# Second attention block: both halves of the head mix written into one bank, back to back, with one reciprocal and one product on VectorE

## The reference, cut to what matters

```python
wq = (q @ wq_w.T + wq_b).reshape(b, t, H, DH)          # H = 16, DH = 8
wk = (k @ wk_w.T + wk_b).reshape(b, t, H, DH)
wv = (v @ wv_w.T + wv_b).reshape(b, t, H, DH)
scores = jnp.einsum('bthd,bshd->bhts', wq, wk) / jnp.sqrt(jnp.float32(DH))
probs = jax.nn.softmax(scores, axis=-1)
attn = jnp.einsum('bhts,bshd->bthd', probs, wv)
return attn.reshape(b, t, d) @ wo_w.T + wo_b
```

## Time and profile before

| | before |
|---|---|
| median of 3 runs | 430.23 us |
| the profiled execution | 430.68 us |
| its span (first to last instruction) | 428.9 us |
| TensorE matmul busy | 383.9 us, 90% |
| VectorE busy | 332.2 us, 77% |
| ScalarE busy | 255.9 us, 60% |
| GpSimd busy | 226.7 us, 53% |
| mean granted TensorE clock | 0.976 |

### The profile page before, as it was taken

How to read it: one execution, slowest core, us unless ns; L and a number is a source line. 1 busy time by engine, 2 the same in 40 slices (tenths; PEclk the granted TensorE clock), 3 DMA queues, 4 the chain that set the end, 5 groups by cost and what they waited for, 6 DMA issues and landing times. The chain is left out here.

```text
span 428.9 us, 10603 instructions
## 1 busy us (share of the span) xinstructions
PE 383.9 (90%) x3641; PEld 282.8 (66%) x3654; DVE 332.2 (77%) x933; ACT 255.9 (60%) x506; POOL 226.7 (53%) x372
## 2 busy tenths in 40 slices
PE   8799989999999999999999999988888887765765
PEld 7356656666666666786578887856666766654554
DVE  3789998999989998885738874665588888866772
ACT  2478757777777777766542224445777676773252
POOL 4575497566666666632300002773788887656021
PEclk9999999999999999999999999999999999975799
DMA  5889999100000000000000000000000000000011
GB/s 160 245 146 136 135 125 127 14 3 2 2 2 2 2 2 2 0 2 2 2 2 0 0 2 2 0 2 2 2 2 3 2 2 2 2 2 0 16 38 49
DMA packets 61284, 13.29 MB, mean 31 GB/s; under 512 B 51488, under 2 KB 60592, under 8 KB 61232
## 3 DMA queue, kind: packets, MB, share of 16 engines
q1 hardware_dynamic: 59776, 11.94, 18.8%
q10 hardware_dynamic: 1328, 0.66, 0.5%
q0 software_dynamic: 128, 0.00, 0.0%
HBM read 11.55 MB, written 1.05 MB: 29 GB/s over the span
## 5 line engine op out<-in xcount | busy, mean ns | idle before, releaser
L397 POOL TENSOR_TENSOR a_rn<-a_ssq,neghalf 128x8 f32<-128x8 f32 x48 | 79.0, 1655 | 30.1 <-DVE a_ssq L996 25.6
L996 DVE TENSOR_REDUCE a_ssq<-q_home 128x8 f32<-128x512 f32 x48 | 32.3, 673 | 6.4 <-ACT q_home L783 6.3
L486 PE MATMUL a_x<-wkv_a,a_kvT 128*128 128x512 f32 x64 | 34.5, 621 | 0.9 <-ACT kv_home L789 0.8
L91 POOL TENSOR_TENSOR moments<-moments,eps_row 128x1 f32<-128x1 f32 x32 | 6.2, 195 | 54.9 <-DVE moments L86 54.6
L789 ACT ACTIVATE kv_home<-a_x,maskcol 128x512 f32<-128x512 f32 x32 | 21.9, 684 | 18.4 <-PE a_x L486 18.4
L1750 DVE TENSOR_REDUCE b_mx<-b_s 128x16 f32<-128x1024 f32 x16 | 19.6, 1225 | 10.4 <-PE b_s L1461 10.3
L1338 POOL TENSOR_TENSOR b_k<-b_ksb,quad 128x256 f32<-128x256 f32 x32 | 19.0, 614 | 14.3 <-ACT b_ksb L1625 14.3
L1015 DVE TENSOR_REDUCE a_mx<-a_s 128x4 f32<-128x512 f32 x32 | 22.0, 686 | 2.0 <-PE a_s L512 1.9
L413 POOL TENSOR_TENSOR a_yr<-a_ymv,eps_row 128x1 f32<-128x1 f32 x16 | 3.1, 192 | 38.0 <-DVE a_ymv L1039 38.0
L801 ACT ACTIVATE kv_home<-a_m,cols 128x512 f32<-128x512 f32 x32 | 22.0, 686 | 0.8 <-PE a_m L500 0.7
L531 PE MATMUL a_m<-kv_home,p_home 128*64 128x65 f32 x512 | 22.0, 228 | 0.3 <-ACT p_home L811 0.3
(11 more groups left out here) (293 smaller groups left out, 1186.7 us busy)
## 6 DMA issues: line engine op xcount, KB each, us to landing
w_gu<-in_L_ffn_Wg_dram SPq DMA_DIRECT2D x4, 512.0 KB, 9.1
w_gu<-in_L_ffn_Wu_dram SPq DMA_DIRECT2D x4, 512.0 KB, 11.1
w_d<-in_L_ffn_Wd_dram SPq DMA_DIRECT2D x8, 256.0 KB, 7.8
out_dram<-xs SPq DMA_DIRECT2D x8, 128.0 KB, 1.8
xs<-in_x_dram SPq DMA_DIRECT2D x1, 640.0 KB, 11.4
cs<-in_ctx_dram SPq DMA_DIRECT2D x1, 640.0 KB, 10.9
wkv_a<-in_L_xattn_Wkv_dram SPq DMA_DIRECT2D x1, 512.0 KB, 8.4
nat<-in_L_ffn_w_dram SPq DMA_DIRECT2D x2, 256.0 KB, 3.1
```

Of the source, the lines that this page charges most:

```text
L397: nc.gpsimd.tensor_tensor(rn[:, tp, i, :], ssq[:, tp, i, :], neghalf[:, 0:H0], ALU.pow)\
L486: nc.tensor.matmul(p_x[:], kvT[:, tp, b * 2 * S:(b + 1) * 2 * S], wkv_a[:, INNER:2 * INNER], start=True, stop=True).then_inc(vproj_done, 1)
L996: nc.vector.tensor_reduce(ssq[:, tp, i, :], sq[:, i, :].rearrange("p (h d) -> p h d", h=H0), AX.X, ALU.add).then_inc(reduced, 1)
```

## The change

Three edits go together. On TensorE, `mix(t, 1)` moves from behind `project` of the next turn to directly behind `mix(t, 0)`, and writes the same bank `p_m`, in the columns behind the first half (2 x 72 = 144 of 512). The waits that guarded `p_y` go: three in `mix(t, 1)`, one in `up`. On VectorE, `attend` waits once, for both halves, and then takes one reciprocal over 16 columns and one product over 128, where it took two of each over 8 and 64.

```diff
             def mix(t, tp, j):
                 pe.wait_ge(prT_ready, 2 * t + j + 1)
                 pe.wait_ge(v_ready, 2 * t + 2)
-                if j == 1:
-                    wait(pe, x_new, t)
-                    wait(pe, hid_ready, t - 3)
-                    wait(pe, att_ready, t)
...
-                        last = nc.tensor.matmul(p_mix[j][b * S:(b + 1) * S, i * W:(i + 1) * W],
+                        last = nc.tensor.matmul(p_m[b * S:(b + 1) * S, n * W:(n + 1) * W],
...
             def up(t, tp):
                 pe.wait_ge(hT_ready, t + 1)
-                pe.wait_ge(att_ready, min(t + 4, NT))
...
                 if s >= 2 and exists(s - 1, NT):
                     project(s - 1, (s - 1) % 2)
-                if exists(s - 3, NT):
-                    mix(s - 3, (s - 3) % 2, 1)
...
                 if exists(s - 2, NT):
                     mix(s - 2, s % 2, 0)
+                    mix(s - 2, s % 2, 1)
...
             def attend(t, tp):
-                o4 = [p[:, 0:HH * W].rearrange("p (n h e) -> p n h e", n=HH, h=2) for p in p_mix]
-                for j in range(2):
-                    dve.wait_ge(mixed, 2 * t + j + 1)
-                    last = nc.vector.reciprocal(rs[:, tp, j * HH:(j + 1) * HH, :], o4[j][:, :, :, DH])
-                last.then_inc(inverse, 1)
+                o4 = p_m[:, 0:HP * W].rearrange("p (n h e) -> p n h e", n=HP, h=2)
+                dve.wait_ge(mixed, 2 * t + 2)
+                nc.vector.reciprocal(rs[:, tp], o4[:, :, :, DH]).then_inc(inverse, 1)
                 dve.wait_ge(inverse, t + 1)
                 wait(dve, aT_done, t - 1)
-                for j in range(2):
-                    n = slice(j * HH, (j + 1) * HH)
-                    last = nc.vector.tensor_tensor(att[:, tp, n].rearrange("p n h e -> p (n h) e"),
-                                                   o4[j][:, :, :, 0:DH].rearrange("p n h e -> p (n h) e"),
-                                                   rs[:, tp, n].rearrange("p n h -> p (n h)").unsqueeze(2)
-                                                   .to_broadcast([P, HP, DH]), ALU.mult)
-                last.then_inc(att_ready, 1)
+                nc.vector.tensor_tensor(att[:, tp].rearrange("p n h e -> p (n h) e"),
+                                        o4[:, :, :, 0:DH].rearrange("p n h e -> p (n h) e"),
+                                        rs[:, tp].rearrange("p n h -> p (n h)").unsqueeze(2)
+                                        .to_broadcast([P, 2 * HP, DH]), ALU.mult).then_inc(att_ready, 1)
```

More of the change, by code:

```diff
@@ L1296, in attention_ffn @@
         p_t, p_m, p_k, p_y = (pb(n) for n in "t m k y".split())
-        p_prob, p_mix, p_out = (p_m, p_t), (p_m, p_y), (p_t, p_m)
+        p_prob, p_out = (p_m, p_t), (p_t, p_m)
         (zeroed, ready, xn_ready, cT_done, xT_done, cT_ready, xT_ready, qkv_done, k_ready, q_ready, v_ready, k4_ready,
```

## The result

The changed kernel took 435.66 us in the median of 4 runs (433.31 to 437.03) against 429.90 us before: a ratio of 1.0126, 95% interval 1.0072 to 1.0180. Run again beside other kernels it gave 1.0103 (1.0053 to 1.0153). It is slower, by 4 to 6 us. The forecast was 436.6, the range 433.2 to 441.0. The profiled execution is 6.3 us longer than the one before: the ring takes 2.9 us of that, about 1.6 us went in a fall of the clock in one turn, 1.4 us were lost at the very start of the span, where the kernels are the same, and 0.4 us at the end of the stage.

The account below looks back on a forecast made before the run. The prediction took a ring of spread_keys, TensorE and ScalarE's key copy, without VectorE, as the bound. Its terms, +8.1 - 1.5 - 0.2 = +6.4 us, gave a 436.6 us median, range 433.2 to 441.0.

Parts of the forecast that it names:

- the ring: Closed chain from spread_keys through TensorE's turn_attention to project, then ScalarE's key copy, back to spread_keys; about 6.1 us a turn.
- Rivals A and B: A: VectorE sets the turn, 428.2 us, chance 0.09. B: half 1 fits TensorE's idle time, 430.2 us, chance 0.05.
- Half 1 ahead of `project`, +8.1 us: On TensorE, half 1 delays project and the next turn by 0.58 us, 14 times: +8.1 us (7.7 to 9.1).
- My lower end, 0.55 for the weight loads: Lower bound on half 1's price per turn on TensorE: the half's weight loads alone, 0.55 us.
- The gap, -1.5 us: Between spread_keys' end and turn_attention: falls to its 0.08 us floor every turn, worth 0 to 1.8 us, 1.5 taken.
- `attend` 0.24 us shorter: On VectorE, one reciprocal and one product take 0.51 us where two of each took 0.75.
- The waits removed and `project`, -0.2 us: On TensorE, removed waits and half 1 covering project's hold by norm_out's copy: -0.2 us in all (0 to -0.5).
- 6.4 to 6.6 us between them: Sign of being right: the 14 starts of spread_keys stand this far apart in steady turns, against 6.0 to 6.2 before.
- my own mark (over 6.1): Sign of being wrong: spread_keys starts spaced 6.1 us or less.
- Rival C, the clock: TensorE's clock falls as well in two or three turns of the stage, slower still: 444 us, chance 0.05.
- my own sign, a clock under 1.00 between 292 and 376 us: Sign of the forecast being wrong and rival C holding: granted clock below 1.00 in that stretch of the profile.
- Only behind longer pauses: Argument against rival C: the clock went to 0.50 only behind longer pauses at the end of the stage.

Follow-up runs that it names:

- run 2: The changed kernel with two reciprocals and two products on VectorE again, behind the one wait; median 436.19 us, ratio 1.0110 to the kernel before.
- run 1: The changed kernel with half 1 of the mix back in its old place behind project; median 429.75 us, ratio 0.9971 to the kernel before.
- run 7: The kernel before, with up's wait for att_ready left out where turn_input already has it; median 431.56 us, ratio 0.9989.
- runs 3: The kernel before, with six of project's seven waits issued ahead of half 0 of the mix; median 431.17 us, ratio 1.0020.
- run 6: The kernel of run 1, without project's six implied waits from the fourth tile on; median 428.37 us, ratio 0.9926 to the kernel before.
- run 9: The changed kernel, without project's six implied waits from the fourth tile on; median 436.93 us, ratio 1.0116 to the kernel before.
- run 11: The changed kernel with turns 3 and 4's filler matmuls moved from ahead of scores to idle time ahead of turn_attention; median 432.63 us, ratio 1.0037.
- run 10: The changed kernel, measured again with nothing altered; median 436.15 us, ratio 1.0103 to the kernel before.

## Why the prediction was right, and where it only came out right

- **What bounds it:** right. The ring of `spread_keys`, TensorE and the key copy is the chain in every profile, and run 2 shows VectorE off it once half 1 has moved. Rivals A and B are out by run 1 against the changed kernel: the move costs 0.30 us a turn.
- **Half 1 ahead of `project`, +8.1 us:** mis-sized. It measured 0.46 us a turn (0.49 in the first three), 6.5 in 14. I took half 0's whole link, 0.58, for half 1; 0.12 of it isn't paid a second time. Where in the link the 0.12 sit, no run shows. My lower end, 0.55 for the weight loads, was no bound either: 32 loads take 1.01, so 16 more add 0.46.
- **The gap, -1.5 us:** right in kind and near in size: 0.09 in each of the 13 turns, 1.7 us. In the kernel before 0.09 us a turn of it would have been won by `up`'s wait alone (run 7); in the changed kernel TensorE idles 0.53 us ahead of `turn_attention`, more than that wait costs.
- **`attend` 0.24 us shorter:** wrong; 0.10 (run 2). It did no harm, since nothing waited for it.
- **The waits removed and `project`, -0.2 us:** the term with the wrong cause. I put the hold down to `norm_out`'s copy. It was the list of six waits, 0.13 to 0.18 us in each turn, about 1.8 us in 14; half 1 covers it (runs 3, 6, 9).
- **The sum:** 6.5 - 1.7 - 1.8 = 3.0 us for the ring, against 6.4 predicted and 2.9 measured by the starts of `spread_keys`. That the total came out at the forecast is luck: what was too much here was made up by clock losses, for which the sum had nothing. I said 6.4 to 6.6 us between them; it is 6.23. By my own mark (over 6.1) the step stands, its size doesn't.
- **Rival C, the clock:** too low at 0.05, and placed wrongly. It isn't an alternative to the forecast but a part of it: 1.55 us in the second turn of both profiles of the changed kernel, 3.8 us in run 11. By my own sign, a clock under 1.00 between 292 and 376 us, it was seen. I looked at the steady turns, where the clock did stay at 1.00 in both profiles of the changed kernel, and not at the early ones, where half 1 was all that TensorE had to do. "Only behind longer pauses" was no margin either: in the kernel before, `turn_attention` at 380.89 stands behind 1.79 us without a matmul and the clock is 0.50 from 382 us on, and the move leaves 1.66.
- What remains of the profiled difference, 1.8 us before and behind the turns, isn't the change's by any run here. In the 12 profiles that first start of `spread_keys` lies between 287.48 and 290.83, with the two latest in the profiles that have a fall of the clock ahead of the stage; what follows the last start is 53.9 to 56.0 us long, in no order of the kernels.

## What to carry to other kernels

Before work is moved to save instructions on another engine, ask of both places whether the chain runs through them: 0.46 us of matmuls were free behind `project` and paid for in full ahead of it. A wait that has long been met is not free where the wait ahead of it has only just let go: count the waits behind the one that is truly waited for, and leave out those that program order implies. When moved work leaves a hole, look at the turns where the hole has nothing else in it.

## What the hardware showed that I had not expected

Six semaphore waits, all met, between two matmuls on TensorE cost about 0.13 us (link 0.35 us with them in run 1, 0.23 without in run 6), and one between two others 0.1 us (run 7). With half 1 between the copy's end and `turn_context` the six cost nothing (turn 6.23 us with and without them, run 9). After 1.66 us without a matmul the granted clock went from 1.00 to 0.50 in the first profile and run 10, and didn't in runs 2 and 9 with the same pause; run 11 fell behind pauses of 0.94 and 0.53 us.
